# Graph network, edge passes: one-hot casts four deep, bank copies moved by one tile, one-hots by VectorE in the first pass, one head of eight weighed by ScalarE

## The reference

```python
# first pass (graph convolution), once
norm = deg_inv_sqrt[src] * deg_inv_sqrt[dst]
out = segment_sum(h[src] * norm[:, None], dst, num_segments=N)

# attention, for each of L = 3 layers, H = 8 heads of HD = 32
kt = _typed_transform(K[src], W_E[l], edge_type)
scores = sum(Q[dst] * kt, axis=-1) / scale * mu[l].T[edge_type]
m = segment_max(scores, dst);  e = exp(scores - m[dst])
w = e / (segment_sum(e, dst) + 1e-10)
agg = segment_sum(V[src] * w[..., None], dst)
```

## Time and profile before

| | us |
|---|---|
| median of 3 runs | 9000.31 (8999.39 to 9012.17) |
| profiled execution | 9019.28, its span 9017.5 |
| PE, DVE, ACT, POOL busy | 6295.3, 4610.5, 3230.8, 4297.5 |
| granted TensorE clock, mean | 0.87 |
| first pass over the edges | 228 to 1527 |
| attention over the edges, layers 0, 1, 2 | 1866 to 3585, 4247 to 5968, 6626 to 8343 |

### The profile page before, as it was taken

The page is one execution under the profiler, slowest core; times in us unless marked ns, Lnnn a source line. Parts: engine busy times, 40 slices in busy tenths (PEclk is TensorE's granted clock), DMA queues, the critical chain, the costliest instruction groups (busy, mean ns, idle before and its releaser), DMA issues. The chain is left out here.

```text
span 9017.5 us, 131863 instructions
## 1 busy us (share of the span) xinstructions
PE 6295.3 (70%) x28156; PEld 4550.1 (50%) x28157; DVE 4610.5 (51%) x11823; ACT 3230.8 (36%) x9690; POOL 4297.5 (48%) x4007
## 2 busy tenths in 40 slices
PE   1566666766767676997666666779876766666990
PEld 1334334654444444887444444468764444444780
DVE  6112123545555555663555555557545555555677
ACT  6566665233333333223333333332333333333222
POOL 0666664355455554225555545533355555554234
PEclk9788888888888888998888888899988888888995
DMA  3343344675555554007555555520375555555002
GB/s 105 111 121 119 117 121 110 192 223 148 147 150 163 149 156 116 29 28 248 172 155 157 148 146 151 152 67 30 110 235 154 153 152 152 153 149 138 27 29 90
DMA packets 599952, 1188.76 MB, mean 132 GB/s; under 512 B 89303, under 2 KB 359087, under 8 KB 599711
## 3 DMA queue, kind: packets, MB, share of 16 engines
q0 software_dynamic: 239984, 774.78, 31.5%
q1 hardware_dynamic: 311491, 372.73, 12.1%
q10 hardware_dynamic: 48364, 39.97, 1.6%
HBM read 980.36 MB, written 213.21 MB: 132 GB/s over the span
## 5 line engine op out<-in xcount | busy, mean ns | idle before, releaser
L1423 POOL DMA_INDIRECT at_kv<-kv_table,at_stage x2496 | 2649.6, 1062 | 2427.4 <-DVE at_wv L1586 1659.5
L1510 PE MATMUL ps<-at_wv,at_hot 128*128 128x264 f32 x4992 | 1800.3, 453 | 636.5 <-DVE ps L1620 302.6
L1456 ACT CAST at_hot_t<-at_hot_t 128x256 f32<-128x256 uint8 x1248 | 505.0, 405 | 3226.1 <-PE ps L1523 1771.8
L1523 PE MATMUL ps<-sums,at_hot_t 128*128 x4992 | 1594.5, 450 | 83.8 <-issue 56.4
L1492 PE MATMUL ps<-zeros_b 128*128 128x264 bf16 x2505 | 781.5, 312 | 929.5 <-ACT sums L1439 698.1
L1510 PEld LDWEIGHTS ps<-at_wv,at_hot 128*128 128x128 f32 x4992 | 925.5, 220 | 986.3 <-issue 520.4
L1568 DVE TENSOR_TENSOR at_prod<-ps,at_kv 128x512 f32<-128x512 f32 x1248 | 859.6, 689 | 1072.2 <-remote 619.1
L1523 PEld LDWEIGHTS ps<-sums,at_hot_t 128*128 128x128 f32 x4992 | 1010.2, 224 | 374.6 <-issue 123.7
L1439 ACT COPY sums<-ps x2499 | 940.8, 376 | 304.8 <-DVE ps L1620 156.4
L703 POOL DMA_INDIRECT gc_rows<-x_scaled,gc_stage x832 | 800.6, 962 | 465.0 <-remote 215.7
L1492 PEld LDWEIGHTS ps<-zeros_b 128*128 128x128 bf16 x2505 | 261.0, 104 | 1467.8 <-ACT sums L1439 1021.1
(11 more groups left out here) (291 smaller groups left out, 8085.0 us busy)
## 6 DMA issues: line engine op xcount, KB each, us to landing
kv_table<-pj_v SPq DMA_DIRECT2D x150, 396.0 KB, 3.3
kv_table<-pj_k SPq DMA_DIRECT2D x150, 384.0 KB, 2.7
at_hot_t<-hot_columns SPq DMA_DIRECT2D x156, 256.0 KB
at_kv<-kv_table,at_stage POOLq DMA_INDIRECT x2496
at_hot<-hot_rows SPq DMA_DIRECT2D x156, 256.0 KB
at_rec<-block_records SPq DMA_DIRECT2D x156, 226.0 KB
pj_x<-x_state ACTq DMA_DIRECT2D x150, 128.0 KB, 2.2
an_x<-x_state SPq DMA_DIRECT2D x75, 256.0 KB, 2.8
```

The costliest lines, as they stand in the source:

```text
L1423: nc.gpsimd.indirect_dma_start(kv[:, 2 * k + j, :], None, g.tab_d.rearrange("t n c -> (t n) c"), bass.IndirectOffsetOnAxis(index, 0)).then ...
L1510: t.matmul(own[j], hot[:, slot % 2, j, :], wv[:, slot % WRING, j, :], start=False, stop=True, skip_group_check=True).then_inc(summed, 1)
L1523: mm = t.matmul(ps[:, slot % QRING, j * D:(j + 1) * D], hot_t[:, slot % 2, j, :], q_rows[j], start=True, stop=True)
```

## The change

- Attention: `at_hot` and `at_hot_t` get four buffers instead of two (`HRING`), and the casts wait for four pairs back. ScalarE's order in a step becomes: copy of the odd tile of pair k-16, cast of the rows, copy of the even tile of pair k-15, cast of the columns, exponentials, weighing. So each even tile's copy comes one step earlier in the order.
- Attention: VectorE weighs seven of the eight heads (`SPLIT`), ScalarE the eighth, with one `Copy` scaled per edge for each tile. It signals `weighed_too`, for which TensorE's sums and GpSimd's gathers wait as well.
- First pass: VectorE makes the one-hots in one comparison (`make_hot`, `is_equal` of minus_place and minus_iota); `dist` and the two `Abs` and the float `Relu` are gone from ScalarE, which casts the finished one-hots to uint8. The turned ones have four banks instead of two, and VectorE copies them two pairs later (`LAG_COPY`). The sum bank copies follow by three tiles instead of eight (`GCN_EVAC`), one ahead of the cast and one behind it.

```diff
...
                 table(g.tab, LOTS, WORDS, 32, 0, 2 * LAG_Q, wrow, UROW, 2 * UROW)
...
-                table(g.tab, LOTS, WORDS, 64, 0, 2 * LAG_EVAC, previous, 512, first_bank)
-                table(g.tab, LOTS, WORDS, 64, LOT, 2 * LAG_EVAC, wrow, UROW, 0)
+                table(g.tab, LOTS, WORDS, 64, 0, LAG_EVAC, previous, 512, first_bank)
+                table(g.tab, LOTS, WORDS, 64, LOT, LAG_EVAC, wrow, UROW, 0)
...
-                table(g.gcn_tab, GCN_LOTS, GCN_WORDS, 64, 0, 2 * GCN_EVAC, previous, 512, first_bank)
-                table(g.gcn_tab, GCN_LOTS, GCN_WORDS, 64, LOT, 2 * GCN_EVAC, wrow, UROW, 0)
+                table(g.gcn_tab, GCN_LOTS, GCN_WORDS, 64, 0, GCN_EVAC, previous, 512, first_bank)
+                table(g.gcn_tab, GCN_LOTS, GCN_WORDS, 64, LOT, GCN_EVAC, wrow, UROW, 0)
...
         need_apart(pool, staged, r + 1)
         for k in range(RING):
             if not first:
-                need_apart(pool, used, RING * (r - 1) + k + 1)
+                for sem in used:
+                    need_apart(pool, sem, RING * (r - 1) + k + 1)
             for j in range(2):
...
-GCN_EVAC = 4
+GCN_EVAC = 3
...
+        TURN_BANKS, CROSS_BANK, LAG_COPY = 4, 4, 2
...
 
-                gather_tiles(nc, pool, g.idx_x, stage, staged, summed, fetch)
+                gather_tiles(nc, pool, g.idx_x, stage, staged, (summed,), fetch)
 
             @block.scalar
             def _(act):
-                def evacuate(n, words, k, j):
-                    w = 2 * (k % LOT_DUOS) + j
+                def evacuate(n, j, words, w):
...
-                def turn(i):
...
-                        n = RING * i + k
+                def turn(i, last=False):
+                    for k in range(2 if last else RING):
+                        n, w = RING * i + k, 2 * (k % LOT_DUOS)
                         if k % LOT_DUOS == 0:
                             words = load_words(nc, g.gcn_tab[64:65], ACT_ENGINE,
-                                               4 * GCN_WORDS * i + (k // LOT_DUOS) * GCN_WORDS,
-                                               EVAC_TOPS)
-                        if not isinstance(n, int) or n >= GCN_EVAC:
-                            evacuate(n - GCN_EVAC, words, k, 0)
-                        if k == 0:
-                            act.copy(place[:, 0], g.minus_place[:, bass.ds(2 * RING * i, 2 * RING)]).then_inc(placed, 1)
-                            act.wait_ge(placed, i + 1)
-                        for j in range(2):
-                            d = act.activation(dist[:, k % 2, j, :], g.iota[:], ACT.Abs, bias=place[:, 0, 2 * k + j:2 * k + j + 1])
-                        d.then_inc(dist_ready, 1)
-                        if not isinstance(n, int) or n >= GCN_EVAC:
-                            evacuate(n - GCN_EVAC, words, k, 1)
-                        need(act, hot_turned, n - RING + 1)
-                        need(act, summed, n - RING + 1)
-                        act.wait_ge(dist_ready, n + 1)
-                        act.activation(hot[:, k], dist[:, k % 2], ACT.Relu, bias=1.0, scale=-1.0).then_inc(hot_ready, 1)
-                        b, u = divmod(k, DUOS)
-                        if u == 0:
-                            need(act, hot8_stored[b], 16 * i)
-                        act.activation(hot8[:, b, u, :], dist[:, k % 2].rearrange("p j n -> p (j n)"), ACT.Relu,
-                                       bias=1.0, scale=-1.0).then_inc(hot8_made, 1)
+                                               4 * GCN_WORDS * i + (k // LOT_DUOS) * GCN_WORDS, EVAC_TOPS)
+                        if not isinstance(n, int) or n >= 2:
+                            evacuate(n - 2, 1, words, w)
+                        if not last:
+                            b, u = divmod(k, DUOS)
+                            act.wait_ge(hot_ready, n + 1)
+                            if u == 0:
+                                need(act, hot8_stored[b], 16 * i)
+                            act.copy(hot8[:, b, u, :], hot[:, k].rearrange("p j n -> p (j n)")).then_inc(hot8_made, 1)
+                        if not isinstance(n, int) or n >= 1:
+                            evacuate(n - 1, 0, words, w + 1)
 
                 act.wait_ge(cleared, 1)
                 turn(0)
                 with act.Fori(1, TURNS) as i:
                     turn(i)
-                for k in range(GCN_EVAC + 1):
-                    if k % LOT_DUOS == 0:
-                        words = load_words(nc, g.gcn_tab[64:65], ACT_ENGINE,
-                                           4 * GCN_WORDS * TURNS + (k // LOT_DUOS) * GCN_WORDS, EVAC_TOPS)
-                    for j in range(2 if k < GCN_EVAC else 1):
-                        evacuate(PAIRS - GCN_EVAC + k, words, k, j)
+                turn(TURNS, last=True)
 
...
                         t.wait_ge(hot_ready, n + 1)
-                        need(t, hot_t8_made, n - 1)
+                        need(t, hot_t8_made, n - TURN_BANKS + 1)
                         for j in range(2):
-                            tr = t.transpose(g.ps[:, TURN_BANK + k % 2, j * P:(j + 1) * P], hot[:, k, j, :], g.ident[:])
+                            tr = t.transpose(g.ps[:, k % TURN_BANKS, j * P:(j + 1) * P], hot[:, k, j, :], g.ident[:])
...
+                def make_hot(i, k):
+                    n = RING * i + k
+                    if k == 0:
+                        need(v, hot_ready, n)
+                        v.tensor_copy(place[:], g.minus_place[:, bass.ds(2 * RING * i, 2 * RING)]).then_inc(placed, 1)
+                        v.wait_ge(placed, i + 1)
+                    need(v, hot_turned, n - RING + 1)
+                    need(v, summed, n - RING + 1)
+                    need(v, hot8_made, n - RING + 1)
+                    v.tensor_tensor(hot[:, k], place[:, 2 * k:2 * k + 2, None].to_broadcast([P, 2, P]),
+                                    g.minus_iota[:, None, :].to_broadcast([P, 2, P]), ALU.is_equal).then_inc(hot_ready, 1)
+
+                def copy_columns(i, k):
+                    b, u = divmod(k, DUOS)
+                    v.wait_ge(hot_turned, RING * i + k + 1)
+                    if u == 0:
+                        need(v, hot_t8_stored[b], 16 * i)
+                    v.tensor_copy(hot_t8[:, b, u, :], g.ps[:, k % TURN_BANKS, 0:GROUP]).then_inc(hot_t8_made, 1)
+
                 def turn(i):
                     for k in range(RING):
-                        b, u = divmod(k, DUOS)
-                        n = RING * i + k
-                        v.wait_ge(hot_turned, n + 1)
-                        if u == 0:
-                            need(v, hot_t8_stored[b], 16 * i)
-                        v.tensor_copy(hot_t8[:, b, u, :], g.ps[:, TURN_BANK + k % 2, 0:GROUP]).then_inc(hot_t8_made, 1)
+                        make_hot(i, k)
+                        if k >= LAG_COPY:
+                            copy_columns(i, k - LAG_COPY)
+                        elif not isinstance(i, int):
+                            copy_columns(i - 1, RING + k - LAG_COPY)
                         if k == AT_ENDS:
                             tile_ends(i)
                         if k == AT_RECORD:
@@ -865,6 +866,8 @@
                 turn(0)
                 with v.Fori(1, TURNS) as i:
                     turn(i)
+                for k in range(RING - LAG_COPY, RING):
+                    copy_columns(TURNS - 1, k)
...
 LAG_SUM = 15
-LAG_EVAC = 16
-LAG_RESCALE = 16
+LAG_EVAC = 31
+SPLIT = 7
+HRING = 4
...
-        hot_t = sb("at_hot_t", [P, 2, 2, P])
+        hot = sb("at_hot", [P, HRING, 2, P])
+        hot_t = sb("at_hot_t", [P, HRING, 2, P])
...
-                gather_tiles(nc, pool, g.idx_kv, stage, staged, weighed, fetch)
+                gather_tiles(nc, pool, g.idx_kv, stage, staged, (weighed, weighed_too), fetch)
...
-                    if now := at(LAG_EVAC):
+                    if now := at(LAG_EVAC // 2 + 1):
                         n, slot, turn = now
-                        evacuate(2 * n, words, w, 2 * turn + slot // DUOS if u == 0 else None)
+                        evacuate(2 * n + 1, words, w)
+
+                    if now := at(LAG_WEIGH):
+                        n, slot, turn = now
+                        par, place = divmod(slot, DUOS)
+                        if place == 0:
+                            act.wait_ge(hot_in[par], 16 * turn + 16)
+                        need(act, summed, 2 * (n - HRING + 1))
+                        act.copy(hot[:, slot % HRING].rearrange("p j e -> p (j e)"), hot8[:, par, place, :]).then_inc(h_cast, 1)
+
+                    if now := at(LAG_EVAC // 2):
+                        n, slot, turn = now
+                        evacuate(2 * n, words, w + 1, 2 * turn + slot // DUOS if slot % DUOS == 0 else None)
 
                     if now := at(0):
                         n, slot, turn = now
                         b = slot // DUOS
                         if u == 0:
                             act.wait_ge(hot_t_in[b], 16 * turn + 16)
```

(38 more changed lines are left out.)

22 lines of the change are left out of this document (9 added, 13 removed).

## The result

The changed kernel takes 8342.8 us (8322 to 8358, four runs) against 9006.2 us of the kernel before (8999 to 9012, four runs): ratio 0.926, interval 0.924 to 0.929. It is 663 us faster. The forecast was 8540, in a range of 7900 to 9060. The profiled execution took 8354.0 us, 665 less than the one of before.

A forecast was written before the change was run, and what follows sets the result against it. Waits bound it: ScalarE and TensorE waiting on each other in turn, plus late completions. 9019.3 - 421 (attention, 2.7 us times 156 blocks) - 40 (first pass) = 8558, 8540 us as median; range 7900 to 9060.

The forecast's parts named there:

- Term 1, the rings: Attention: four-deep cast buffers open the ScalarE-TensorE loop, 0.63 us in each of four steps, 2.5 us a block (0 to 6.0).
- Step 3 and step 7, counted as one more together: Attention block: these two hold the same loop plus a load of address words; together counted as one step's 0.63 us.
- Step 0, counted as plain: Attention block: steps 0, 1 and 2 counted as plain, each falling from 2.71 to 2.08 us, a gain of 0.63.
- Term 3, ScalarE's share: Attention: ScalarE weighs head 7, two instructions of 0.20 us a pair; its step becomes 1.6 us, hidden under TensorE's 2.08.
- Terms 4 and 5: Attention: VectorE's shorter weighing gains 0.2 us a block; new waits of TensorE and GpSimd for ScalarE's weighing cost 0.
- GpSimd found waiting for ScalarE's weighing: Attention: sign named for a wrong prediction; it would say buffers come free a step later than counted.
- H: Attention, experiments' theory: ScalarE's late weighing holds GpSimd, fewer gathers begin, the queue runs dry sooner and late spells shorten.
- First pass (-40 us, between -260 and +89): First pass over edges: GpSimd sets it, so less ScalarE work gives 0; forecast -40 us if some TensorE waits go.
- A: Attention: TensorE's completions withheld until the gather queue runs dry, so faster casts gain nothing; 9000 us, chance 0.22.
- B: Attention: idle spells arise from the two engines' alternation and vanish; 7340 us, or 8000 with half gone; chance 0.15.
- C: First pass: VectorE's comparison stretches gathers, 83 us, plus 26 behind records; slower, 9180 us with late completions undoing the gain; chance 0.14.
- V: Attention, experiments' theory: VectorE's shorter weighing, 0.07 us each, is why ScalarE's weighing of a head shortens the late spells.

The follow-up runs named there:

- rings and copies: Kernel before, cast buffers four deep, ScalarE's copies moved: 8586.2 us, ratio 0.942, late completions; in time read from changed kernel without ScalarE's weighing: 7241.4 us, ratio 0.918.
- the rings alone: Kernel before with only the attention's two cast buffers four deep, completions in time: 7336.6 us against 7892.2, ratio 0.930.
- the copies alone: Kernel before with ScalarE's new order (copies and cast of the rows moved), buffers two deep, completions in time: 7229.3 us against 7892.2, ratio 0.916.
- the whole change held tighter: Changed kernel where GpSimd's gather also waits for both sums of the pair that used its buffer, completions in time: 7207.0 us against 7878.3, ratio 0.914.
- the first pass alone: Kernel before with only the new first pass and its tables, completions in time: 7928.3 us, ratio 1.005, slower by 36 us.

## Why the prediction was right, and where not

**The bound.** The loop of ScalarE and TensorE was the bound that could be taken away, as the idle of L1456 said: it opened. I read too much into that idle, though: of its 3226.1 us only 1771.8 ended with L1523, and 1156.1 had no named releaser.

**The number.** 663 us against 466 forecast: within the range, but made up otherwise. On the late chip rings and copies give 516 us (421 less 31 said), the share of ScalarE 235 (31 said), and the first pass nothing (40 said); that these come to 751 and not 663 is the difference between the two sets of runs, 9102 - 8351 against 9006 - 8343. The loop's gain was foreseen in kind. That the share's gain fell on the same side was luck.

**Term 1, the rings (2.5 us a block).** The mechanism holds, the size was off, and the credit was misplaced. In time, rings and copies give 4.5 us a block, the rings alone 3.8 and the copies alone as much as both. "Step 3 and step 7, counted as one more together" was the term that failed: step 3 gave 2.5 us by itself, step 4 gave 0.6, and step 7 lost 0.2 (it waits for the rescale, L1620). Step 0, counted as plain, gave 0.2. The trace of before could have shown it, in the very block of the earlier trace rows that meets no late completion. Its sums in steps 2, 3 and 4 begin here:

```profile
4434.75 0.61 PE L1510 MATMUL ps<-at_wv,at_hot 128*128 128x264 f32 x2
...
4437.44 0.61 PE L1510 MATMUL ps<-at_wv,at_hot 128*128 128x264 f32 x2
...
4442.30 0.68 PE L1510 MATMUL ps<-at_wv,at_hot 128*128 128x264 f32 x2 [1.16 <-ACT at_hot L1477]
```

Step 2 is plain, 2.69 us; step 3 takes 4.86, and its end waits for ScalarE's cast of the rows. Of the long means of that kernel, 7.07 and 6.26 us, step 2's excess did belong to the late completions, step 3's only in part. On the late chip rings and copies are worth 516/156 = 3.3 us a block, so about 1.2 us of the 4.5 is taken back there.

**Term 3, ScalarE's share.** 321 ns instead of 200; ScalarE's step is then, by the estimate of 1.2 for the rest, 1.2 + 0.64 = 1.84 us, still under TensorE's 1.98. That it is hidden was right, by a small margin: with the share and completions in time (the whole change held tighter) steps 1 and 2 take 1.98 and 2.00 us.

**Terms 4 and 5, VectorE's 0.2 us and the new waits at nothing.** Together 31 us by my sum; measured 235 on the late chip. VectorE's own part, measured where completions are in time, is some 0.3 us a block, about 50 us. The rest, some 185 us, came with shorter spells. I had listed "GpSimd found waiting for ScalarE's weighing" as a sign that the prediction is wrong. It was found, 375.8 us of it, and the kernel was faster. That the wait itself does this (H) is argued from the fewer gathers in a spell, not shown.

**First pass (-40 us, between -260 and +89).** Measured -2 where completions are late, +14 in its trace and +36 in the total where they are not. The reasoning (GpSimd sets it, ScalarE's work doesn't matter) was right, the -40 was hope. The upper bound of +89 does not follow from its terms either: 83 and 26 make 109.

**Rivals.** A, the late completions take it back: in part, 1.2 of 4.5 us by comparing the two kinds of chip. B, the spells go with the loop: no, 208 became 176 to 188. C, the comparison stretches the gathers: the effect exists but is 16 ns a gather, 13 us, where I had bounded it by 83. By the Trainium skill, "SBUF — State Buffer", section Who interferes with whom, writing gather descriptors is inferred not to be held up by a VectorE instruction with two SBUF inputs; the 16 ns beside a comparison of 417 ns agree with that nearly, not wholly, and the attention's gathers of 1.50 us beside a VectorE without gaps, where its shortest take 0.95, do not. The measurement decides: beside such a VectorE a gather is held up.

**The cost of late completions** I had put at 6.3 us a block and 200 us of the first pass. The two kinds of chip give 1719 - 1425 = 294 us a pass, 5.7 us a block, and some 1120 us in the total (9006 against 7878 to 7892). Nothing in the trace of before told me that it belongs to the chip.

**Signs named beforehand.** Plain steps at 2.05 us (2.1 said), first pass 1297 us with 100 spells (1290 with 95 said): met. Clears waiting under 300 us for ScalarE: 339.3, missed. Passes at 1580 us: 1502, missed.

**Open.** What makes completions late on some chips; whether H or V; what rings or order alone give where completions are late; 22 us of the first pass alone. Where completions are late only one other version that computes the same ran (rings and copies), and it is slower than the changed kernel. Where they are in time the changed kernel itself wasn't run, and the versions with the new order lie within 0.5% of each other, the first pass old or new.

## What to carry to other kernels

When two engines wait for each other once per step, write down the order of the instructions on each and move the one that the other engine needs ahead of those that can wait; deeper buffers open the loop too, but here, where completions are in time, the order alone was worth as much as both. Look at the long steps of a period for the same loop before giving their length to another cause: a step in which both engines also load words had the whole of both in series. Before comparing two runs, compare the kernel before beside each of them: here it differed by 14% between chips. Whether an engine with a backlog is worth slowing where its transfers delay others (H) these runs do not show.
